# Attention in one kernel: products with V two blocks behind the scores, maximum jobs issued one by one

## The reference

```python
scores = jnp.einsum('bhqd,bhkd->bhqk', q, k) / math.sqrt(hd)   # B=1, H=16, S=4096, hd=16
scores = jnp.where(causal, -jnp.inf, scores)
attn = jax.nn.softmax(scores, axis=-1)
attn_out = jnp.einsum('bhqk,bhkd->bhqd', attn, v)
...
x = x + s * g        # s: attention layer, g: silu of the experts' layer
```

## Time and profile before

| | |
|---|---|
| median of 3 runs | 2322.44 us |
| span of the profiled execution | 2321.9 us |
| TensorE matmuls | 2217.7 us, 96% |
| VectorE | 1960.4 us, 84% |
| ScalarE | 1454.6 us, 63% |
| GpSimd | 214.7 us, 9% |
| reductions of the maximum pass, line 1155 | 1332.2 us, x2176 |
| exponentials, line 1128 | 1075.3 us, x1152 |

### The profile page before, as it was taken

The page is one execution under the profiler, slowest core; times in us unless marked ns, Lnnn a source line. Parts: engine busy times, 40 slices in busy tenths (PEclk is TensorE's granted clock), DMA queues, the critical chain, the costliest instruction groups (busy, mean ns, idle before and its releaser), DMA issues. The chain is left out here.

```text
span 2321.9 us, 48508 instructions
## 1 busy us (share of the span) xinstructions
PE 2217.7 (96%) x18612; PEld 1338.0 (58%) x18612; DVE 1960.4 (84%) x3755; ACT 1454.6 (63%) x1778; POOL 214.7 (9%) x287
## 2 busy tenths in 40 slices
PE   3999987999999999999999999999999989999998
PEld 2889883444444444444444444444444438998998
DVE  7888977889999988999999989988888817777887
ACT  3534320277777777777777777778777775555443
POOL 3110101010021300000000000000000000000544
PEclk9999995699999999999999999999999999999999
DMA  6232337012101111110001130000210015453222
GB/s 157 95 126 106 111 127 124 6 34 68 33 13 44 52 45 35 34 45 12 12 12 35 34 103 12 12 22 1 32 22 4 4 47 193 151 153 98 85 95 81
DMA packets 138295, 143.68 MB, mean 62 GB/s; under 512 B 36168, under 2 KB 101320, under 8 KB 137976
## 3 DMA queue, kind: packets, MB, share of 16 engines
q1 hardware_dynamic: 132624, 129.68, 19.6%
q0 software_dynamic: 3072, 8.39, 1.1%
q10 hardware_dynamic: 2432, 3.28, 0.5%
HBM read 88.17 MB, written 51.02 MB: 60 GB/s over the span
## 5 line engine op out<-in xcount | busy, mean ns | idle before, releaser
L1155 DVE TENSOR_REDUCE attn_MX<-psB 128x1 f32<-128x512 f32 (+3 forms) x2176 | 1332.2, 670 | 158.9 <-PE psB L969 103.2
L1128 ACT ACTIVATE attn_PB<-psB 128x1024 f32<-128x1024 f32 (+3 forms) x1152 | 1075.3, 953 | 381.4 <-PE psB L1023 313.0
L969 PE MATMUL psB<-KS,attn_QS 52*128 52x512 f32 (+3 forms) x1152 | 327.8, 453 | 26.4 <-DMA KS<-picking_rows 17.7
L1045 PE MATMUL psB<-attn_PB,V 128*32 128x256 f32 (+4 forms) x4016 | 332.8, 403 | 1.5
L1045 PE MATMUL psB<-attn_PB,attn_V 128*32 128x256 f32 (+5 forms) x3560 | 322.4, 434 | 1.6 <-ACT attn_PB L1128 0.6
L969 PE MATMUL psB<-attn_KS,attn_QS 52*128 52x512 f32 (+3 forms) x1152 | 282.9, 408 | 2.7 <-DVE attn_MX L1155 1.4
L1023 PE MATMUL psB<-attn_QS,KS 52*128 52x512 f32 (+3 forms) x1152 | 279.7, 469 | 0.1
L1023 PE MATMUL psB<-attn_QS,attn_KS 52*128 52x512 f32 (+3 forms) x1152 | 273.9, 461 | 5.4 <-ACT attn_PB L1128 3.4
L969 PEld LDWEIGHTS psB<-KS,attn_QS 52*128 52x128 f32 x1152 | 188.2, 199 | 97.4 <-DVE attn_MX L1155 67.5
L1023 PEld LDWEIGHTS psB<-attn_QS,attn_KS 52*128 52x128 f32 x1152 | 110.9, 184 | 229.0 <-issue 109.8
L1023 PEld LDWEIGHTS psB<-attn_QS,KS 52*128 52x128 f32 x1152 | 111.5, 184 | 213.9 <-issue 140.6
(11 more groups left out here) (239 smaller groups left out, 3096.1 us busy)
## 6 DMA issues: line engine op xcount, KB each, us to landing
W<-in_w SPq DMA_DIRECT2D x18, 1024.0 KB, 5.6
qk_parts<-proj_PT SPq DMA_DIRECT2D x32, 512.0 KB, 2.8
attn_QS<-qk_parts SPq DMA_DIRECT2D x192, 64.0 KB
v_rows<-proj_VA SPq DMA_DIRECT2D x32, 256.0 KB, 2.0
attn_KS<-qk_parts SPq DMA_DIRECT2D x96, 64.0 KB, 2.6
KS<-qk_parts SPq DMA_DIRECT2D x90, 64.0 KB, 3.0
XN<-in_x SPq DMA_DIRECT2D x8, 512.0 KB, 9.3
rows_by_place<-proj_ZR SPq DMA_DIRECT2D x32, 128.0 KB, 2.4
```

The costliest lines, as they stand in the source:

```text
L969: mm = nc.tensor.matmul(ps[:, bank, at * width:(at + 1) * width], QS[rows, i % 4, b, j * P:(j + 1) * P], KS[w][rows, b, kc * CH:kc * CH + ...
L1045: mm = nc.tensor.matmul(ps[32 * h:32 * (h + 1), PV, cols], V[w][:, kb, 32 * h:32 * (h + 1)], PB[:, u % RING, h, cols], start=(k == 0 and f ...
L1128: nc.scalar.activation(PB[:, u % RING, 2 * pair:2 * pair + 2, r * P:CH], ps[:, 2 * (s % 2):2 * (s % 2) + 2, r * P:CH], ACT.Exp, scale=HD * ...
L1155: nc.vector.tensor_reduce(MX[:, m % 4, first:first + 2 * n - 1:2, kc], ps[:, MB + off % 3, 0:n * w].rearrange("p (h n) -> p h n", h=n), AX ...
```

## The change

BEHIND = 2: the product of block u - 2, not u - 1, is issued with the scores of block u. It is always cut in two halves, one behind each pair of scores. The new jobs of a block are shared out over four places: behind the first pair of scores, behind the first half product, behind the second pair, behind the second half. With 4 new jobs one stands in each place, with 3 the last place is empty, with 2 the second and the fourth. Jobs on the diagonal chunk are still issued two at a time. ScalarE copies the sums of a step one block later, behind the exponentials of the next step's second block. RING stays 3. The product is issued as 1148 halves and, for the last two blocks, 2 whole ones.

```diff
-AHEAD = 2
+AHEAD, BEHIND = 2, 2
...
-                for i in range(LS):
-                    for k in range(len(units[i])):
-                        new = upto[i][k] - at
-                        halves = behind is not None and new > 3
-                        done = at
-                        scores(i, k, 0)
-                        ask(done + (2 if halves else (new + 1) // 2))
-                        if halves:
-                            mid = (units[behind[0]][behind[1]][1] * P + CH) // 2
-                            weigh(*behind, 0, mid)
-                        scores(i, k, 1)
-                        if k == rows_at(i) and i + 1 < LS:
+                def weigh_half(u, second):
+
+                    if u < 0:
+                        return
+                    i, k = flat[u]
+                    mid = (units[i][k][1] * P + CH) // 2
+                    weigh(i, k, *((mid, CH) if second else (0, mid)))
+
+                for u, (i, k) in enumerate(flat):
+                    done = at
+                    share = lambda n: min(upto[i][k], done + (n * (upto[i][k] - done) + 3) // 4)
+                    for pair in range(2):
+                        scores(i, k, pair)
+                        if pair == 1 and k == rows_at(i) and i + 1 < LS:
                             max_rows(i + 1, s_rows(i), s_rows(i) - 1, i + 2)
-                        ask(done + 4 if halves else upto[i][k])
-                        if behind is not None:
-                            weigh(*behind, mid if halves else 0, CH)
-                        behind = (i, k)
-                        ask(upto[i][k])
-                        if i == LS - 1 and k == 1:
-                            transposes()
-                weigh(*behind, 0, CH)
+                        ask(share(2 * pair + 1))
+                        weigh_half(u - BEHIND, pair == 1)
+                        ask(share(2 * pair + 2))
+                    if i == LS - 1 and k == 1:
+                        transposes()
+                for u in range(len(flat) - BEHIND, len(flat)):
+                    i, k = flat[u]
+                    weigh(i, k, 0, CH)
...
-                        if k == 0 and i > 0:
+                        if k == BEHIND - 1 and i > 0:
                             sums(i - 1)
```

More of the change, by code:

```diff
@@ L1066, in _ @@
                             max_rows(0, 0, None, 1)
-                behind = None
                 at = j_base[AHEAD]
+                flat = [(i, k) for i in range(LS) for k in range(len(units[i]))]
                 def ask(count):
```

## The result

The changed kernel takes 2412.64 us, the median of 4 runs (2400.67 to 2426.77), against 2323.02 us before in the same comparison: a ratio of 1.0377, interval 1.0347 to 1.0406. The forecast was 2404 us, range 2345 to 2480, slower. The profiled execution of after has a span of 2421.1 us.

The account below looks back on a forecast made before the run. TensorE (1.23 us a cycle) and VectorE (1.25) were taken as level in four-job blocks, TensorE as the bound in three-job ones; 31 + 55 + 14 - 9 - 9 = +82 us on 2322 gave 2404 us, range 2345 to 2480.

Parts of the forecast that it names:

- rival 2: Only the splits cost and the order in the row halves costs nothing: +13, up to +40 us, about 2345; chance 7%.
- Splits: Blocks without a split before: two product halves and a second turn cost 0.17 us each, 185 blocks, 31 us.
- Row halves: TensorE groups between products: a job meeting the first score in its own row half loses its pair; 55 + 14 us.
- the bad order: Even-head job ahead of a score pair, in the first score's row half: cycle 1.48 us, against 1.22 behind an odd head.
- the lower price: Least cost of a product-to-product cycle with an even-head job ahead of the scores: 1.46 us; 1.48 was taken.
- S starts a whole step later: Score pair (S) behind a maximum job (J) in the same row half: 0.23 us from J to S with weights loaded.
- the upper price: Most that a cycle with an even-head job ahead costs: 1.65 us, with 0.42 from job to scores.
- Good order, down to VectorE's rate: 128 four-job blocks that start on an even head fall from 2.58 to 2.51 us at best: -9 us.
- No room in the buffers: Rival: third buffer free too late, exponentials wait for half a product; 115 us on top, about 2519; chance 2%.
- Waits of products for exponentials: Products two blocks behind give back part of an 18.3 us wait: 9 us taken, bounds 0 and 18.
- VectorE's waits over 180 us: Sign: waits of VectorE's reductions for TensorE rise from 128 us to over 180.
- the two sorts of four-job blocks: Sign: four-job blocks come in two sorts, 2.5 and about 2.96 us; all at 2.5 would be wrong.

Follow-up runs that it names:

- halves alone: Kernel before with every product cut in two halves, still one block behind, jobs still issued two at a time: 2401.46 us, ratio 1.0349.
- the run with whole products: Changed kernel, but blocks with at most 3 new jobs keep the product whole at the block's end: 2388.45 us, ratio 1.0258.
- the run with singles alone: Kernel before, one behind with its own splits, but jobs issued one by one in four-job blocks off the diagonal: 2341.78 us, ratio 1.0085.
- the run with every group in the bad order: Changed kernel, but the first matmul of each score pair lies in the row half of the job ahead: 2420.00 us, ratio 1.0382.
- the run with whole products there: Changed kernel, but in the 16 blocks of the first step products are issued whole at the block's end: 2384.90 us, ratio 1.0256.
- the run with the rows first: Changed kernel, but in four-block steps SP moves the next step's row maxima ahead of the stores of the sums: 2382.53 us, ratio 1.0246.
- Two behind alone: Kernel before with products two blocks behind and the sums' copy one block later, nothing else: 2372.11 us, ratio 1.0156.
- the runs with both edits: Changed kernel with row maxima moved first in four-block steps and whole products in the first step: 2347.02 us, ratio 1.0081.

## Why the prediction was right, and where not

**The total and the sign were right**, 2404 against 2412.6. That the total came so close was luck. The sum behind it was not right: it held a cost that does not exist, it had no term for the clock, and the two errors met. At full clock the kernel did what rival 2 says (only the splits cost, +13 to +40, given 7%): +33 or a little more, with four-job blocks all near 2.5 us, the sign that the forecast itself had named for being wrong.

**Splits: right for the three-job blocks when nothing else changes, too small in sum.** The forecast had +31 us in turns and lone groups and a three-job block at 2.48 us. Measured at full clock: 2.49 and 2.45 with halves alone. The stretch with halves everywhere is 1490 us or a little more against 1442, so about +50, since narrow two-job blocks go from 2.08 to 2.48 and not by 0.17, and narrow three-job ones from 2.35 to 2.63. After has 2.52 and 2.46, but there the splits are not shown to be the cause: the run with whole products and the run with singles alone have 2.52 and 2.43, 2.55 and 2.42 without a split in these blocks. Each of the two edits brings a three-job block to about 2.5 us, and both together bring no more. In the narrow two-job blocks it is the splits: 2.52 in after, 2.21 with the products whole.

The Trainium skill (TensorEngine Tiling (Array Packing), Key Properties) says that a change of tiling mode drains TensorE. It stood on the right side. The run with halves everywhere agrees with it: about 50 us for 204 products split anew, some 0.25 us each, in which the drain is not told apart from the second group's own time.

**Blocks with five jobs: no term.** The forecast says "Diagonal jobs are still issued in pairs and cost as now" and prices no block with five new jobs. They cost 13 us more.

**Row halves: wrong.** The step "if the J ahead is an even head, it meets S lower in its own half: no pair is left" carried 55 + 14 us. The cycle is 1.23 us in both orders, and the run with every group in the bad order took no longer. The step that the lower price rested on, "S starts a whole step later", does not happen: with an even head ahead, job and first score both start at 1005.62. The row on which the upper price rested holds a wait: the weights of its scores had waited 0.23 us for an exponential, so I took a distance with a wait in it for a distance between neighbours:

```profile
1577.36 0.19 PEld L1023 LDWEIGHTS psB<-attn_QS,attn_KS 52*128 52x128 f32 x2 [0.23 <-ACT attn_PB L1128]
```

As I read the rows, a job or scores fresh behind a product are followed by the next in 0.33 us whatever its place, and this hides the extra stream; the rows' modelled ends can't show the streams themselves.

**Good order, down to VectorE's rate: right in size, wrong in kind.** Both kinds of four-job block fell to 2.45 to 2.50, not the good kind alone; but the gain was lent: the run with singles alone is 17 us slower than before.

**The clock: missing.** No term of the sum and no rival held it, though the page's clock line before the change showed two low slices that end just where the second pass starts. It is the largest term, 57 to 65 us: about half at the start, where the split blocks keep the clock at 1.2 GHz until 518 us of the trace and not 452 (28 us by the run with whole products there), about half in the dips (30 us by the run with the rows first, stalls included).

**SP's queue: the sentence that failed is "SP's store waits for that copy and lands long before the buffer is wanted again".** True of the buffer, and beside the point: behind the stores in the same queue stands the move of the row maxima. The wait itself is 8 us in four places; what it sets off is more.

**No room in the buffers: rightly ruled out**, no exponential waits for a product. **Waits of products for exponentials: no gain seen.** Two behind alone is 1440 us at full clock against 1442, so about 2 of the 9 us that I took.

The signs named in advance: VectorE's waits over 180 us came (226). The waits of maximum loads for VectorE were to fall from 53.7 and rose to 203; the two sorts of four-job blocks, 2.5 and 2.96, did not come. Either of these alone would have told that the 55 us term was wrong while the total was right.

## What to carry to other kernels

Before an instruction or a semaphore is moved by one block, list everything behind it in each queue that waits for it, and test the shortest step first: a delay that long steps swallow ends in the open in a step of four blocks. In this kernel TensorE's clock was lost in a loop that had just started at half clock and at the end of the shortest steps, and 14 products kept whole there were worth 28 us, as much as some hundred of them elsewhere at 0.25 us each. Look at the clock line there first. And when a total comes out right, check the terms: here 69 us of a cost that does not exist stood in for some 60 us of one that was not thought of.

## What the hardware showed that was not expected

**Time follows the granted clock from run to run.** The four runs of the changed kernel: 2400.67 and 2402.44 us at a mean clock of 0.946, 2422.84 at 0.937, 2426.77 at 0.935. The same binary loses 26 us between the ends, with 0.011 of clock: about half of the time spent at 1.2 GHz is lost. The spread of a kernel's runs can thus be read as clock, and of the runs with both edits one at 0.938 took 2411 us where its neighbours at 0.970 took 2347.

**TensorE can be busy all the time and still be held at half clock.** From 456 to 514 us after has matmuls in 58.00 of 58.00 us, by their modelled ends, and the clock is 0.50; with whole products it is granted in full from about 455 us on. Both ran at half clock up to there; what differs is that the products issued in the first 16 blocks come in one piece, and with them the jobs in pairs. The halves alone do it on the kernel before, where the jobs stay in pairs. It is not that split blocks are slower at half clock: a wide block with three jobs takes 4.33 us split (after, from 462.50 us) and 4.33 us whole (the run with whole products in the first step, from 449.09 us). Why the clock came back at 518 us in after and at 514 with the first step split was not tried; both moments are in the second step. Why the split form holds the clock down is open. Some falls came without a wait ahead of them: before the fall at 773 us with halves alone and the one at 1395 us with the rows first, no gap of TensorE in the 25 us ahead is over 0.3 us. So the idle wait is one cause and not the only one.
